# A two-stage convolution block on one core: far products as squares, one more product by minimal filtering, and a regrouped end

## What is computed

```python
spot = jnp.concatenate([ones, patches], axis=-1)            # 10 values
feat = (spot[..., :, None] * spot[..., None, :])            # 100 products
out = jnp.einsum('bcyxf,ocf->boyx', feat, filters)          # 32 in, 32 out channels
x = x + out
```

## Time and profile before

| what | us |
|---|---|
| three runs | 298.53, 299.28, 300.03 |
| the profiled execution | 300.92 |
| its span, first to last instruction | 299.2 |
| TensorE busy | 275.4 |
| VectorE busy | 255.4 |
| ScalarE busy | 87.7 |
| GpSimd busy | 29.6 |

### The profile page before, as it was taken

The page is one execution under the profiler, slowest core; times in us unless marked ns, Lnnn a source line. Parts: engine busy times, 40 slices in busy tenths (PEclk is TensorE's granted clock), DMA queues, the critical chain, the costliest instruction groups (busy, mean ns, idle before and its releaser), DMA issues.

```text
span 299.2 us, 13594 instructions
## 1 busy us (share of the span) xinstructions
PE 275.4 (92%) x6464; PEld 129.7 (43%) x6464; DVE 255.4 (85%) x218; ACT 87.7 (29%) x135; POOL 29.6 (10%) x86
## 2 busy tenths in 40 slices
PE   0499999999999999999999999999999999997990
PEld 0123443443444434354447477435335355654440
DVE  1799699997999979799999999992999999997213
ACT  4530205979439789818200000002200000000000
POOL 7922930000010000000000000000000000000000
PEclk9999999999999999999999999999999999999996
DMA  6975000000000000000000000058000000000077
GB/s 190 377 180 114 2 2 3 4 3 4 2 2 4 2 4 2 2 4 3 2 4 4 2 4 2 4 105 180 3 4 2 2 4 2 4 2 4 6 139 140
DMA packets 19462, 11.45 MB, mean 38 GB/s; under 512 B 18000, under 2 KB 18128, under 8 KB 19280
## 3 DMA queue, kind: packets, MB, share of 16 engines
q1 hardware_dynamic: 14768, 9.06, 11.9%
q10 hardware_dynamic: 4640, 1.53, 2.2%
HBM read 6.40 MB, written 4.19 MB: 35 GB/s over the span
## 4 chain that ended last, share of the span: by engine, by line
PE 58%; DVE 25%; issue 8%; ACT 3%; DMA 3%; SPq 1%; DVEq 0%
PE acc L1074 41%; PE acc L1117 15%; DVE product L944 8%; DVE product L932 3%; DVE stats L775 3%; ACT raw L540 3%; DMA raw<-in_x 3%; DVE arena L820 2%; PE acc L1168 2%; DVE product L941 1%; DVE raw L944 1%; DVE plane L793 1%; DVE raw L853 1%; DVE arena L842 1%; DVE arena L703 1%
## 5 line engine op out<-in xcount | busy, mean ns | idle before, releaser
L1074 PE MATMUL acc<-product,weight 32*32 32x512 f32 (+1 forms) x3072 | 127.9, 604 | 2.1 <-DVE arena L842 1.8
L1074 PEld LDWEIGHTS acc<-product,weight 32*32 32x32 f32 (+1 forms) x3072 | 64.0, 110 | 62.7 <-issue 45.0
L944 DVE TENSOR_TENSOR product<-plane 128x4096 f32<-128x4096 f32 x18 | 78.9, 4427 | 0.1
L1074 PE MATMUL acc<-raw,weight 32*32 32x512 f32 (+1 forms) x960 | 45.1, 603 | 0.0
L1117 PE MATMUL acc<-product,middle 32*64 32x512 f32 (+1 forms) x576 | 31.5, 598 | 0.3 <-issue 0.3
L1074 PEld LDWEIGHTS acc<-raw,weight 32*32 32x32 f32 (+1 forms) x960 | 20.5, 112 | 20.3 <-issue 15.6
L775 DVE BATCH_NORM_STATS2 stats<-raw 128x6 f32<-128x512 f32 x32 | 19.7, 681 | 3.7 <-DMA raw<-in_x 3.6
L1074 PE MATMUL acc<-product,arena 32*32 32x512 f32 (+1 forms) x448 | 22.2, 604 | 0.0
L540 ACT ACTIVATE raw<-arena 32x512 f32<-32x512 f32 x32 | 21.8, 682 | 0.5
L570 ACT ACTIVATE arena<-acc 128x2048 f32<-128x2048 f32 x2 | 3.8, 1881 | 61.2 <-PE acc L1074 61.2
L540 ACT ACTIVATE raw<-product 32x512 f32<-32x512 f32 x28 | 19.0, 680 | 2.7 <-DVE product L703 2.3
(11 more groups left out here) (130 smaller groups left out, 239.4 us busy)
## 6 DMA issues: line engine op xcount, KB each, us to landing
raw<-in_x SPq DMA_DIRECT2D x8, 512.0 KB, 9.5
out<-raw SPq DMA_DIRECT2D x16, 128.0 KB, 2.9
arena<-in_L_conv_filters SPq DMA_DIRECT2D x4, 400.0 KB, 6.4
out<-raw SPq DMA_DIRECT2D x16, 64.0 KB, 2.4
out<-raw ACTq DMA_DIRECT2D x16, 64.0 KB, 2.6
arena<-in_L_conv_w ACTq DMA_DIRECT2D x4, 100.0 KB, 3.6
w_in<-in_L_conv_w ACTq DMA_DIRECT2D x2, 36.0 KB, 1.8
w_in<-in_L_conv_w SPq DMA_DIRECT2D x2, 36.0 KB, 2.2
```

The lines of the kernel that those rows point to most:

```text
L944: nc.vector.tensor_tensor(both_halves(g, u), plane_halves(g), plane_halves(g, PRODUCTS[k][0] * PITCH + PRODUCTS[k][1]), ALU.mult)\
L1074: return nc.tensor.matmul(acc[32 * s:32 * (s + strips), j, r, :], weights[32 * r:32 * r + 32, t:t + strips, :] .rearrange("p t c -> p (t c ...
```

## The change

Four things are changed.

1. Unit 9 (FAR_ROW, displacement (0,2)) is no longer a product made by VectorE. The linear side streams hold the difference of the left and the right neighbour of each pixel; ScalarE squares them (`square_far_row`). Since ab = (a² + b² - (a-b)²)/2, GpSimd scales the weights of this unit by -0.5 and subtracts them from the square's outer taps. In group 0 this is done in place in raw0.
2. In group 1 the diagonal product (unit 7, DIAGONAL) is done by minimal filtering: a sum for both halves with `diagonal_sum`, and the side streams `diagonal_left` and `diagonal_right`. It takes 2 + 2 + 2 rounds where it took 8. The sums of NEXT and DIAGONAL come after the mix rounds, the cross sum is kept before the sum, and the buffers' homes and TensorE's order in group 1 are laid out anew.
3. The last rounds of units 14 and 15 for the odd half are put in another order, and so are the two blocks of the end (unit 17 first, then 16; in the second block the reverse).
4. In stage one `make_ring` comes after `finish_odd(0)`, and ScalarE copies out one image of the odd half before `keep_whole(1)`.

```diff
+FAR_ROW, DIAGONAL, DIAGONAL_SIDES = 9, 7, LAST_UNIT + 1
...
-             {LINEAR: 0, SQUARE: "raw1", SQUARE_MIXED: 1, NEXT: 2, LINEAR_SIDES: 3, SQUARE_SIDES: 0, NEXT_SIDES: 1,
-              7: "raw1", 8: 2, 9: 3, 10: 0, 11: 1, 12: "raw1", 13: 2, 14: 3, 15: 0, 16: 1, 17: "raw1"})
+             {LINEAR: 0, SQUARE: "raw1", SQUARE_MIXED: 1, NEXT: 2, LINEAR_SIDES: 0, SQUARE_SIDES: 1, NEXT_SIDES: "raw1",
+              DIAGONAL: 3, DIAGONAL_SIDES: 2, 8: 3, 9: 0, 10: 1, 11: "raw1", 12: 2, 13: 3, 14: 0, 15: 1, 16: "raw1",
+              17: 2})
...
 # gpsimd, after the weights' sums
+            last.then_inc(halved, 1)
+            pool.wait_ge(halved, 1)
+            far_row = sums[:, FIRST1[FAR_ROW - 5]:FIRST1[FAR_ROW - 5] + 3, :]
+            nc.gpsimd.tensor_scalar(far_row, far_row, -0.5, None, ALU.mult).then_inc(halved, 1)
+            pool.wait_ge(halved, 2)
+            for a in (FIRST1[0], FIRST1[0] + 6):
+                last = nc.gpsimd.tensor_tensor(sums[:, a:a + 3, :], sums[:, a:a + 3, :], far_row, ALU.subtract)
             last.then_inc(sums_ready, 1)
...
 # scalar
+            def square_far_row(g):
+                wait_used(act, g, LINEAR_SIDES)
+                nc.scalar.activation(both_halves(g, FAR_ROW), both_halves(g, LINEAR_SIDES), ACT.Square)\
+                    .then_inc(far_row_ready, 1)
...
+            spread(0, 1, (0,))
             keep_whole(1)
-            spread(0, 1, range(GROUP - 1))
+            spread(0, 1, range(1, GROUP - 1))
...
             normalise(3)
+            square_far_row(0)
             spread_offset()
             square(1)
+            keep_cross(1)
             keep_sum(1)
-            keep_cross(1)
+            square_far_row(1)
...
 # vector
+            def diagonal_left(g):
+                of_product(g, "diagonal", 0, (1, -1), (0, 0), 1)
+
+            def diagonal_right(g):
+                of_product(g, "diagonal", 1, (1, 0), (0, 0), 1)
...
             turn_edges()
+            finish_odd(0)
             make_ring()
-            finish_odd(0)
             halve(1, "step")
...
-            multiply(0, 9)
             multiply(0, 10)
             mix(0)
...
             multiply(1, NEXT)
             evict(0, 1)
+            multiply(1, DIAGONAL)
             linear_left(1)
             linear_right(1)
             square_left(1)
             square_right(1)
             next_left(1)
             next_right(1)
-            for u in range(7, 10):
-                multiply(1, u)
+            diagonal_left(1)
+            diagonal_right(1)
+            multiply(1, 8)
             mix(1)
...
 # tensor, group 1
-                    pe.wait_ge(stream_made, made(g, "next"))
-                    column(0, stream_pixels(g, NEXT, 0), every_row, next_sum, False, False, PAIRS)
                     mixed_unit(g, 0, "linear", SINGLES)
                     mixed_unit(g, 0, "square", SINGLES)
-                    column(0, stream_pixels(g, NEXT, 0), every_row, next_sum, False, True, SINGLES)\
-                        .then_inc(shared_done, 1)
                     pe.wait_ge(evicted, 2 * GROUP)
                     mixed_unit(g, 1, "linear", SINGLES, start=True)
                     mixed_unit(g, 1, "square", SINGLES)
                     mixed_unit(g, 1, "linear", PAIRS).then_inc(unit_used, 1)
                     mixed_unit(g, 1, "square", PAIRS, stop=True).then_inc(unit_used, 1)
+                    diagonal_rows = rows_of(PRODUCTS[DIAGONAL - 5])
+                    wait_made(g, NEXT)
+                    column(0, stream_pixels(g, NEXT, 0), every_row, next_sum, False, False, PAIRS)
+                    wait_made(g, DIAGONAL)
+                    column(0, stream_pixels(g, DIAGONAL, 0), diagonal_rows, diagonal_sum, False, False, PAIRS)
+                    column(0, stream_pixels(g, NEXT, 0), every_row, next_sum, False, False, SINGLES)
+                    column(0, stream_pixels(g, DIAGONAL, 0), diagonal_rows, diagonal_sum, False, True, SINGLES)\
+                        .then_inc(shared_done, 1)
                     pe.wait_ge(shared_kept, 3)
+                    side_unit(g, 1, "linear", SINGLES, start=True)
+                    side_unit(g, 1, "linear", PAIRS)
+                    pe.wait_ge(shared_kept, 4)
                     side_unit(g, 0, "linear", PAIRS, start=True)
+                    side_unit(g, 0, "linear", SINGLES).then_inc(unit_used, 1)
+                    side_unit(g, 0, "square", SINGLES)
+                    side_unit(g, 1, "square", SINGLES)
                     side_unit(g, 0, "square", PAIRS)
...
+                    side_unit(g, 0, "diagonal", SINGLES)
+                    side_unit(g, 1, "diagonal", SINGLES)
+                    side_unit(g, 0, "diagonal", PAIRS)
+                    side_unit(g, 1, "diagonal", PAIRS).then_inc(unit_used, 1)
+                    in_pairs = True
-                for u in range(7, LAST_UNIT if g == 0 else 14):
+                for u in (range(7, LAST_UNIT) if g == 0 else range(8, 14)):
...
                     wait_made(g, 14)
                     taps1(g, 0, 14, PAIRS)
-                    taps1(g, 1, 14, PAIRS)
                     taps1(g, 0, 14, SINGLES)
                     wait_made(g, 15)
                     taps1(g, 0, 15, SINGLES, True).then_inc(half_done, 1)
-                    taps1(g, 1, 14, SINGLES).then_inc(unit_used, 1)
-                    taps1(g, 1, 15, SINGLES, True).then_inc(half_done, 1)
-                    wait_made(g, 16)
+                    taps1(g, 1, 15, SINGLES)
+                    taps1(g, 1, 14, SINGLES)
+                    taps1(g, 1, 14, PAIRS, True).then_inc(half_done, 1)
+                    wait_made(g, 17)
                     pe.wait_ge(added, 1)
-                    whole_taps(16, 0, SINGLES, start=True)
-                    wait_made(g, 17)
+                    whole_taps(17, 0, PAIRS, start=True)
                     whole_taps(17, 0, SINGLES)
-                    whole_taps(17, 0, PAIRS, stop=True).then_inc(half_done, 1)
+                    whole_taps(16, 0, SINGLES, stop=True).then_inc(half_done, 1)
                     pe.wait_ge(added, 2)
-                    whole_taps(17, 1, PAIRS, start=True)
+                    whole_taps(16, 1, SINGLES, start=True)
                     whole_taps(17, 1, SINGLES)
-                    whole_taps(16, 1, SINGLES, stop=True).then_inc(half_done, 1)
+                    whole_taps(17, 1, PAIRS, stop=True).then_inc(half_done, 1)
```

More of the change, by code:

```diff
@@ L80 @@
 LAST_UNIT = N_PRODUCTS + 4
+FAR_ROW, DIAGONAL, DIAGONAL_SIDES = 9, 7, LAST_UNIT + 1
 UNIT_HOME = ({LINEAR: 1, SQUARE: 3, SQUARE_MIXED: 0, NEXT: 2, LINEAR_SIDES: "raw0", SQUARE_SIDES: 1,
               7: 3, 8: 0, 9: "raw0", 10: 1, 11: 2, 12: 3, 13: 0, 14: "raw0", 15: 1, 16: 2, 17: 3},
-             {LINEAR: 0, SQUARE: "raw1", SQUARE_MIXED: 1, NEXT: 2, LINEAR_SIDES: 3, SQUARE_SIDES: 0, NEXT_SIDES: 1,
-              7: "raw1", 8: 2, 9: 3, 10: 0, 11: 1, 12: "raw1", 13: 2, 14: 3, 15: 0, 16: 1, 17: "raw1"})
+             {LINEAR: 0, SQUARE: "raw1", SQUARE_MIXED: 1, NEXT: 2, LINEAR_SIDES: 0, SQUARE_SIDES: 1, NEXT_SIDES: "raw1",
+              DIAGONAL: 3, DIAGONAL_SIDES: 2, 8: 3, 9: 0, 10: 1, 11: "raw1", 12: 2, 13: 3, 14: 0, 15: 1, 16: "raw1",
+              17: 2})
 USED = ([LINEAR, SQUARE_MIXED, LINEAR_SIDES, SQUARE_SIDES, NEXT] + list(range(7, LAST_UNIT)),
-        [LINEAR, SQUARE_MIXED, LINEAR_SIDES, SQUARE_SIDES, NEXT_SIDES] + list(range(7, LAST_UNIT)))
+        [LINEAR, SQUARE_MIXED, LINEAR_SIDES, SQUARE_SIDES, NEXT_SIDES, DIAGONAL_SIDES] + list(range(8, LAST_UNIT)))
 MADE = (["square sum", "linear cross", "square cross", "linear left", "next", "square left", "linear right",
[L94 to L97, removed]
+         "square right", 7, 8] + list(range(10, LAST_UNIT + 1)),
+        ["linear sum", "linear cross", "square sum", "square cross", "next", DIAGONAL, "linear left", "linear right",
+         "square left", "square right", "next left", "next right", "diagonal left", "diagonal right", 8]
+        + list(range(10, LAST_UNIT + 1)))
+UNIT_OF = {"linear": (LINEAR, LINEAR_SIDES), "square": (SQUARE_MIXED, SQUARE_SIDES), "next": (None, NEXT_SIDES),
+           "diagonal": (None, DIAGONAL_SIDES)}
 def shift_index(ey, ex):
@@ L923, in of_product @@
             def of_product(g, name, half, one, other, sides):
-                source = SQUARE if name == "square" else NEXT
+                source = {"square": SQUARE, "next": NEXT, "diagonal": DIAGONAL}[name]
                 if source == SQUARE:
@@ L928, in of_product @@
                 else:
-                    dve.wait_ge(stream_made, made(g, "next"))
+                    dve.wait_ge(stream_made, made(g, "next" if source == NEXT else DIAGONAL))
                 u = UNIT_OF[name][sides]
@@ L1242, in side_unit @@
                 pe.wait_ge(stream_made, made(g, name + (" right" if j else " left")))
+                if name == "diagonal":
+                    a = FIRST1[DIAGONAL - 5] + 2 * j
```

(23 more changed lines are left out.)

23 lines of the change are left out of this document (16 added, 7 removed).

## The result

The changed kernel takes 297.41 us (median of 11 runs, 296.02 to 298.75) against 299.28 (11 runs, 297.43 to 300.09): ratio 0.9943, 95% interval 0.9917 to 0.9970. In a later batch of runs it was 297.5 against 299.85, ratio 0.9909 (0.9887 to 0.9932). So it is 1.9 to 2.4 us faster. The forecast was 296.6, 2.7 us faster.

A forecast was written before the change was run, and what follows sets the result against it. A chain sets the end: TensorE, VectorE's gapless list behind its wait for LINEAR, TensorE's last blocks, the store. The last blocks start 2.7 us earlier, all else 0: 299.28 becomes 296.6 us, range 295.9 to 297.5.

The forecast's parts named there:

- LINEAR's earlier release: Group 1: LINEAR free 2.86 us earlier, 205.76 for 208.62; VectorE's wait for it falls from 5.40 to 2.7 us.
- VectorE's list behind it: Group 1, behind LINEAR's release: 62.0 us of work for 61.85; the last blocks start 2.7 us earlier, at 270.2.
- TensorE's rounds: Group 1 up to the last blocks: 73 rounds for 75, 1.98 us less; TensorE ready at 269.5 for 271.1.
- the new order of units 14 and 15: Last rounds of units 14 and 15, odd half: the same rounds, no gain or loss.
- a change from singles to pairs and back: TensorE's rounds: some 0.2 us each; about two more in group 1's new order, 0.4 us.
- Who is last: Start of the last blocks: VectorE stays last, by 0.7 us; TensorE's wait for L842 shrinks from 1.8 to 0.7.
- Group 0: Product 9 off VectorE in group 0: between 0 and 0.3 us, taken as 0.
- the seam: Reordered ring and copies before stage two: 0 taken; at worst 1.3 us lost, at best 0.3 won.
- the end: Order of the two last blocks: the same rounds, 0 within 0.5 us either way.
- an earlier start of stage two: Sign of error: stage two was to start still at 91.8; a start elsewhere would show the prediction wrong.
- GpSimd: Added work on the weights: three operations and two waits, at most 0.5 us each, hidden; worst case 0.5 us on the end.
- The in-place square: ScalarE, group 0: 4.31 us, or 5.5 by element; VectorE waits 2.7 us before mix(0). Slower rival: 302.8, chance 0.05.

The follow-up runs named there:

- add_first: Changed kernel with VectorE's even-half addition ahead of unit 17's product and TensorE's last blocks beginning with unit 16: 296.32 us, in another batch 295.94.
- far_only: Kernel before with only the far products as squares in both groups and GpSimd's weight scaling, all TensorE rounds kept: 297.78 us, ratio 0.9924.
- end_undone: Changed kernel with the last rounds of units 14 and 15 and the two last blocks in the order of the kernel before: 297.22 us.
- far1_on_vector: Changed kernel with group 1's far product made by VectorE again, between unit 8 and the mix, without the square: 304.66 us.
- diagonal_late: Changed kernel with group 1's diagonal product behind the linear side streams, so behind VectorE's wait for LINEAR: 303.73 us.
- seam_only: Kernel before with the changed kernel's seam and nothing else: 299.39 us against 299.78, ratio 0.9993.

## Why the prediction was right

It was right in mechanism and direction: VectorE's list behind LINEAR's release sets the start of the last blocks, before and after. The forecast gain of 2.7 us was 0.8 us too large against the first pair of medians (1.9 us), 0.3 against the second (2.4) and 0.4 in D (2.3). The measured 297.41 lies just inside the forecast's own range of 295.9 to 297.5. One term, TensorE's, came out right by luck, as told below.

- **LINEAR's earlier release.** Forecast 10.4 us into the group, measured 204.77 - 194.47 = 10.30. VectorE's wait: forecast 2.7, measured 2.52.
- **VectorE's list behind it.** Forecast 62.0 us, measured 267.25 - 204.77 = 62.48. This is the mis-sized term. Eight half streams take 222.89 - 204.77 = 18.12 us, not 17.64. The side streams of NEXT and of DIAGONAL are written to wait until the pair before them is made; each of these two pairs starts 4.59 us after the last, where it is 4.41 without that wait (204.77 to 209.18), and unit 8, which waits in the same way, 4.53. I had priced half streams from a row in which none waits on its neighbour. So D is 75.2 for my 74.8.
- **TensorE's rounds.** I had TensorE ready 74.1 us into the group, and add_first, where nothing else is last, shows 74.04. That is luck, since two errors cancel. I took TensorE to be ready at 75.7 before, from the listed wait of 1.8 us; far_only shows 75.0 or less. And I put the new order of units 14 and 15 at nothing, where end_undone shows that it costs TensorE 0.7 us. My price of 0.2 us for a change from singles to pairs and back was also rough: by starts, the last single round before pairs takes 1.59 to 1.75 us and the last pair round before singles 0.98 to 1.03, while the first two singles after pairs take 0.87 to 0.94 and not 1.10.
- **Who is last.** I had VectorE last before and after. far1_on_vector shows it from one side (a product more on VectorE's list costs 4.36 us of D), far_only and add_first from the other (with less ahead of the addition, TensorE is last). diagonal_late does not show it, because TensorE is last there.
- **What the parts are worth.** I did not price them apart, and the sum hid this: the squares alone give 2.1 us of E, the diagonal by minimal filtering next to nothing on top of it (0.1), since the two rounds it saves turn into a wait. With the early addition that wait goes, another 1.2 us.
- **Group 0, the seam, the end:** forecast 0, measured 0 within what these runs tell (for TensorE alone the end's order costs 0.7 us, hidden). I had named an earlier start of stage two as a sign of error; it came (90.45 for 91.83), but the kernel before shows the same in a second profile (90.59). The sign was badly chosen, because one profile can't carry it.
- **GpSimd.** Forecast at most 0.5 us for each added operation; measured 2.38 and 1.23 twice. The first started at 39.86, inside VectorE's L693 (39.09 to 41.93), and ended 0.3 us after it. In diagonal_late, where VectorE had only short instructions left by then, the same operation took 0.46 us. By the rule of the Trainium skill (SBUF — State Buffer, "Who interferes with whom") the later of two such instructions, one of VectorE with two inputs in SBUF and one of GpSimd that reads SBUF, is held up; the rows agree. VectorE did not lose by it: L693 took 2.84 us, but the same operation (L671) took 2.53 and 2.79 in the two profiles of the kernel before and 2.84 in seam_only, which have no added operations. My bound for the first was off five times. No cost of it shows on the path: ScalarE still idled 0.63 us ahead of the column edges, and group 1 starts at 194.47, where the profiles without the added operations have 194.13 to 195.40.
- **The in-place square** was cheaper than feared (3.70 us), so `mix(0)` waited 1.85 us and not 2.7.

## What to carry to other kernels

When two engines are nearly full, find which one is last at the point that releases the end, and count the list that stands behind its last wait; what shortens another list turns into a wait there. A rearrangement of that list can be worth over half of what the saved arithmetic is: the addition pulled ahead of a product gave 1.2 us of E, after 2.2 for the whole change. A listed wait of TensorE understates how early it was ready; compare the starts of rounds with and without the wait. Judge an edit of 2 us by the distance between two marks inside one execution, not by the span: here that distance repeats to 0.06 us, while the spans of one kernel differ by 1.3 us.

## What I had not expected of the hardware

A listed wait of TensorE of 1.1 us (the changed kernel) or 1.8 us (the kernel before) left the granted clock at 1.00. After one of 4.24 us and one of 5.49 us the rows show it at 0.50 (1.2 GHz). So VectorE's lateness had a second price in these two: far1_on_vector pays 1.4 us for it in the blocks, diagonal_late 2.6 us in its sum rounds.

A pair round costs 0.85 to 0.96 us. A single round, for the same work of the array, costs 1.04 to 1.11 us within a run of singles, but the first two behind pairs cost no more than a pair round (208.95 to 209.84 above is 0.89), and the last one before pairs costs 1.6 us or more. A change of form can thus cost nearly as much as a round: one more on the way to the blocks cost TensorE 0.7 us. These prices are from the starts of rounds in group 1 up to the last blocks, read in the kernel before, the changed kernel, far_only, add_first and end_undone.
